# q and k projected into 32-row groups per head, split in place, with the scores in pairs of row groups

## What is computed

```
h = group_norm(x, 32 groups of 4 channels) * gn_w + gn_b
q, k, v = wq @ h + bq, wk @ h + bk, wv @ h + bv
attn = softmax(q_head.T @ k_head * scale)      # 256 x 256 per head
x = wp @ (v_head @ attn.T, heads joined) + bp + x
```

## Time and profile before

| | |
|---|---|
| runs (us) | 115.32, 118.06, 115.12; median 115.32 |
| span of the profiled execution (us) | 112.7; its own time is not reported beside it |
| median of the runs less the span (us) | 2.6 |
| busy TensorE, VectorE, ScalarE (us) | 99.7, 77.9, 78.4 |
| TensorE instructions | 774 matmuls, each with a weight load |

### The profile page before, as it was taken

One profiled execution on the slowest core, in us unless ns is written; L12 is line 12 of the kernel. 1 busy time (PEld: TensorE's weight loads), 2 busy tenths in 40 slices (PEclk: granted clock), 3 DMA queues, 4 the chain that ended last, 5 costly groups with the idle time before them and its releaser, 6 DMA issues.

```text
span 112.7 us, 2178 instructions
## 1 busy us (share of the span) xinstructions
PE 99.7 (88%) x774; PEld 80.1 (71%) x774; DVE 77.9 (69%) x192; ACT 78.4 (70%) x168; POOL 7.9 (7%) x17
## 2 busy tenths in 40 slices
PE   6999689979969998599999899979998898789891
PEld 6998468756955967378877678768977565579770
DVE  5467789273992879826699357997869516786862
ACT  4387569998677937989828996377999995024520
POOL 8421000000001000010000100010000000102000
PEclk9999999999999999999999999999999999999998
DMA  2950000000000000000000000000000000000011
GB/s 65 333 214 0 0 0 6 0 0 0 3 9 0 0 0 0 0 0 6 0 0 0 0 6 0 0 0 0 6 0 0 0 0 9 0 3 0 0 47 47
DMA packets 1882, 2.12 MB, mean 19 GB/s; under 512 B 336, under 2 KB 1232, under 8 KB 1872
## 3 DMA queue, kind: packets, MB, share of 16 engines
q1 hardware_dynamic: 1584, 1.84, 4.8%
q10 hardware_dynamic: 288, 0.15, 0.6%
HBM read 1.73 MB, written 0.26 MB: 18 GB/s over the span
## 4 chain that ended last, share of the span: by engine, by line
PE 58%; ACT 20%; DVE 14%; issue 4%; DVEq 0%; ACTq 0%
ACT probs L668 9%; PE ps_o L563 9%; PE ps_t L550 9%; ACT q_heads L658 8%; PE ps_w L492 7%; PE ps_o L469 6%; DVE neg_max L761 6%; PE ps_w L520 4%; PE ps_w L510 4%; PE ps_w L511 3%; PE ps_m L498 2%; DVE q_heads L755 2%; PE ps_m L537 2%; PE ps_m L477 2%; PE ps_m L609 2%
## 5 line engine op out<-in xcount | busy, mean ns | idle before, releaser
L761 DVE TENSOR_REDUCE neg_max<-ps_w 128x2 f32<-128x512 f32 x48 | 31.0, 685 | 6.8 <-PE ps_w L520 6.7
L668 ACT ACTIVATE probs<-ps_t 128x512 f32<-128x512 f32 x48 | 27.5, 597 | 4.1 <-PE ps_t L550 3.3
L550 PE MATMUL ps_t<-q_heads,k_pairs 128*128 128x256 f32 x96 | 20.8, 313 | 3.1 <-ACT probs L668 1.6
L520 PE MATMUL ps_w<-k_pairs,q_heads 128*128 128x256 f32 x96 | 20.4, 314 | 1.8 <-DVE neg_max L761 0.8
L658 ACT ACTIVATE q_heads<-ps_m 1x256 fp32r<-1x256 f32 x48 | 17.9, 373 | 5.0 <-PE ps_m L537 4.1
L550 PEld LDWEIGHTS ps_t<-q_heads,k_pairs 128*128 128x128 f32 x96 | 14.1, 189 | 7.0 <-ACT q_heads L658 4.3
L520 PEld LDWEIGHTS ps_w<-k_pairs,q_heads 128*128 128x128 f32 x96 | 13.9, 189 | 5.5 <-issue 2.4
L510 PE MATMUL ps_w<-qk_high,select 128*128 128x256 f32 x48 | 12.9, 300 | 0.9 <-DVE qk_low L726 0.5
L563 PE MATMUL ps_o<-probs,v_heads 128*32 128x256 f32 x192 | 12.8, 385 | 0.9 <-ACT probs L668 0.9
L511 PE MATMUL ps_w<-qk_low,select 128*128 128x256 f32 x48 | 11.8, 279 | 0.0
L423 POOL TENSOR_TENSOR grp<-grp,const 128x1 f32<-128x1 f32 x8 | 4.5, 558 | 93.8 <-DVE grp L715 93.8
(11 more groups left out here) (62 smaller groups left out, 130.2 us busy)
## 6 DMA issues: line engine op xcount, KB each, us to landing
w<-in_w SPq DMA_DIRECT2D x4, 256.0 KB, 4.9
xs<-in_x SPq DMA_DIRECT2D x2, 128.0 KB, 3.1
selections<-in_selections SPq DMA_DIRECT2D x1, 256.0 KB, 4.0
out<-xs SPq DMA_DIRECT2D x4, 64.0 KB, 1.6
const<-in_constants ACTq DMA_DIRECT2D x1, 137.0 KB, 3.1
vec<-in_vectors ACTq DMA_DIRECT2D x1, 12.0 KB, 3.5
```

Source lines behind the costliest of these rows:

```text
L520: last = mm(ps_w[w_slot[step]][:, qc * T:(qc + 1) * T], q_heads[b][:, i, qc * CHUNK:(qc + 1) * CHUNK], k_pairs[b][:, i // 2, :], start=Tru ...
L550: last = mm(dst, k_pairs[b][:, pair, keys], q_heads[b][:, i, :], start=True, stop=True)
L668: nc.scalar.activation(probs[:, i, :, :].rearrange("p c t -> p (c t)"), src, ACT.Exp, scale=SCALE).then_inc(exps_done, 1)
L761: nc.vector.tensor_reduce(neg_max[b][:, i // 2, :, QUAD * (i % 2)], ps_w[w_slot["scores", l, b, i]][:, :].rearrange("p (c t) -> p c t", c= ...
```

## The change

Instead of one q and one k projection there are two of each (`SETS`), on weights whose columns are repeated: a set holds four heads, each in its own group of 32 rows, and the 16 rows of a head stand in it twice. q is split in place: ScalarE writes the rounded value in the second 16 rows and zero in the first (`mask_q`), and VectorE subtracts that from q (`split_q`), which leaves the full value, rounded, in the first 16 rows and the remainder in the others. k is split into a high and a low tile as before, per set. The placing matmuls, their stores and the selection matrices are gone.

The scores of two heads are now one step of 8 matmuls of 32 rows, which alternate between two row groups and two PSUM banks (high and low part of k, two query halves). The scores by keys are a step of 12 such matmuls, where the last two of each half multiply a row of ones with the stored maxima. The maxima of four heads are turned and stored together, in one store of 128 partitions. There is one ring of five PSUM banks, `probs` exists per image, v is stored by ScalarE, and the plan's table has other times; `fold_bias` is no longer in `LANDED`.

```diff
-WORK, SLOTS = 3, 2
+RING = 5
...
-LANDED = {("moments", 0, 0, 0): 3., ("scale_w", 0, 0, 0): 4.5, ("group_means", 0, 0, 0): 4.5,
-          ("variance", 0, 0, 0): 5.4, ("fold_bias", 0, 0, 0): 6.6, ("moments", 0, 1, 0): 5.8}
+LANDED = {("moments", 0, 0, 0): 3.5, ("scale_w", 0, 0, 0): 4.7, ("group_means", 0, 0, 0): 4.4,
+          ("moments", 0, 1, 0): 5.6}
...
+                for n in range(SETS):
+                    for kind, before in (("mask_q", "project"), ("round_k", "project"),
+                                         ("split_q", "mask_q"), ("split_k", "round_k")):
+                        step(kind, n, (before, n), *[(kind, n - 1)] * n)
+                    for kind in ("mask_q", "round_k"):
+                        needs[kind, l, b, n].append(("add_bias", l, 0, 0))
+                    step("turn_max", n, ("store_v", 0), *[("row_max", PER * n + j) for j in range(PER)],
+                         *[("store_max", n - 1)] * n)
+                    step("store_max", n, ("turn_max", n))
...
+                step("project_v", 0, ("project", SETS - 1))
+                for p in range(PAIRS):
+                    step("scores", p, ("split_q", p // 2), ("split_k", p // 2), *[("scores", p - 1)] * min(p, 1))
+                    step("scores_t", p, ("store_max", p // 2), *[("scores_t", p - 1)] * min(p, 1))
+                    for h in (2 * p, 2 * p + 1):
+                        step("row_max", h, ("scores", p), *[("row_max", h - 1)] * min(h, 1))
+                        step("exps", h, ("scores_t", p), *[("exps", h - 1)] * min(h, 1))
...
+            banks = emptied_by(step)
+            for j in range(len(banks)):
+                if len(ring) + j >= RING:
+                    awaited.append(ring[len(ring) + j - RING])
...
+                        for n, first in enumerate((W_Q[l], W_K[l])):
+                            ring_free(step, n)
+                            mm(slot(step, n)[:, 0:T], ws[l][:, first + i, :], hn[b][:, :],
+                               start=True, stop=True).then_inc(qk_projected, 1)
...
-                elif kind in ("place_q", "place_k"):
-                    k = int(kind == "place_k")
-                    pe.wait_ge(qk_split, nth("split", l, b, k))
-                    if l == 0:
-                        pe.wait_ge(select_ready, (i + 1) * PAIRS // STACKS)
-                    ring_free(step)
-                    for n in range(2):
-                        dst = ps_w[w_slot[step]][:, n * T:(n + 1) * T]
-                        pair = 2 * i + n
-                        mm(dst, select[:, pair, 2 * k, :], qk_high[b][:, k, :], start=True, stop=False)
-                        last = mm(dst, select[:, pair, 2 * k + 1, :], qk_low[b][:, k, :], start=False, stop=True)
-                    last.then_inc(k_placed if k else q_placed, 1)
...
+                    s = i // 2
+                    pe.wait_ge(q_ready, nth("split_q", l, b, s))
+                    pe.wait_ge(k_ready, nth("split_k", l, b, s))
+                    for j in range(2):
+                        ring_free(step, j)
                     for qc in range(NCH):
-                        last = mm(ps_w[w_slot[step]][:, qc * T:(qc + 1) * T],
-                                  q_heads[b][:, i, qc * CHUNK:(qc + 1) * CHUNK], k_pairs[b][:, i // 2, :],
-                                  start=True, stop=True)
+                        for n, keys in enumerate((k_high, k_low)):
+                            for j in range(2):
+                                r = QUAD * (2 * (i % 2) + j)
+                                last = mm(slot(step, j)[:, qc * T:(qc + 1) * T],
+                                          q_split[b][r:r + QUAD, s, qc * CHUNK:(qc + 1) * CHUNK],
+                                          keys[b][r:r + QUAD, s, :], start=(n == 0), stop=(n == 1))
...
-                    pe.wait_ge(max_done, nth("row_max", l, b, 2 * i + 1))
+                    pe.wait_ge(max_done, nth("row_max", l, b, PER * (i + 1) - 1))
...
+                    s = i // 2
+                    pe.wait_ge(max_stored, nth("store_max", l, b, s))
+                    if l == 0:
+                        pe.wait_ge(ones_ready, 1)
+                    for j in range(2):
+                        ring_free(step, j)
...
+                        for n, part in enumerate((k_high, k_low)):
+                            for j in range(2):
+                                r = QUAD * (2 * (i % 2) + j)
+                                mm(slot(step, j)[:, kc * T:(kc + 1) * T], part[b][r:r + QUAD, s, keys],
+                                   q_split[b][r:r + QUAD, s, :], start=(n == 0), stop=False)
+                        for j in range(2):
+                            r = QUAD * (2 * (i % 2) + j)
+                            last = mm(slot(step, j)[:, kc * T:(kc + 1) * T], ones[r:r + 1, :],
+                                      max_rows[b][r:r + 1, s, :], start=False, stop=True)
...
+                elif kind == "mask_q":
+                    act.wait_ge(bias_ready, nth("add_bias", l, 0))
+                    act.wait_ge(qk_projected, 2 * nth("project", l, b, i) - 1)
+                    nc.scalar.activation(q_low[b][:, i, :], slot(("project", l, b, i), 0)[:, 0:T], ACT.Identity,
+                                         bias=bias_low[:, l, i:i + 1], scale=low_rows).then_inc(q_masked, 1)
+                elif kind == "round_k":
+                    act.wait_ge(bias_ready, nth("add_bias", l, 0))
+                    act.wait_ge(qk_projected, 2 * nth("project", l, b, i))
+                    nc.scalar.activation(k_high[b][:, i, :], slot(("project", l, b, i), 1)[:, 0:T], ACT.Identity,
+                                         bias=bias[:, l, K_BIAS + i:K_BIAS + i + 1]).then_inc(k_rounded, 1)
...
-                elif kind == "store_q":
-                    act.wait_ge(q_placed, nth("place_q", l, b, i))
-                    if l == 0:
-                        act.wait_ge(zeros_ready[b], 1)
-                    src = ps_w[w_slot["place_q", l, b, i]][0:HALF, :].rearrange("p (n t) -> p n t", n=2)
-                    nc.scalar.activation(q_heads[b][0:HALF, PER * i:PER * (i + 1):2, :], src,
-                                         ACT.Copy).then_inc(q_stored_even, 1)
-                elif kind == "store_k":
-                    act.wait_ge(k_placed, nth("place_k", l, b, i))
-                    dst = k_pairs[b][:, 2 * i:2 * i + 2, :].rearrange("p n t -> p (n t)")
-                    nc.scalar.activation(dst, ps_w[w_slot["place_k", l, b, i]][:, :], ACT.Identity,
-                                         bias=ones_rows).then_inc(k_stored, 1)
...
-                    for odd in range(2):
-                        row = HALF * odd + MAX_ROW
-                        last = nc.scalar.activation(q_heads[b][row:row + 1, 2 * i + odd, :],
-                                                    m[QUAD * odd:QUAD * odd + 1, 0:T], ACT.Copy)
-                    last.then_inc(max_stored, 1)
+                    nc.scalar.activation(max_rows[b][:, i, :], m[:, i * T:(i + 1) * T],
+                                         ACT.Copy).then_inc(max_stored, 1)
...
+                    link(tt(bias[:, l, :], slot(step_of_fold(l))[:, 0:NBIAS], vec[:, l, BQ:BV + 1], ALU.add))
+                    ts(bias_low[:, l, :], bias[:, l, Q_BIAS:Q_BIAS + SETS], low_rows, None,
+                       ALU.mult).then_inc(bias_ready, 1)
...
+                elif kind == "split_q":
+                    dve.wait_ge(q_masked, nth("mask_q", l, b, i))
+                    stt(out=q_split[b][:, i, :], in0=slot(("project", l, b, i), 0)[:, 0:T],
+                        scalar=bias[:, l, Q_BIAS + i:Q_BIAS + i + 1], in1=q_low[b][:, i, :].bitcast(F32),
+                        op0=ALU.add, op1=ALU.subtract).then_inc(q_ready, 1)
+                elif kind == "split_k":
+                    dve.wait_ge(k_rounded, nth("round_k", l, b, i))
+                    stt(out=k_low[b][:, i, :], in0=slot(("project", l, b, i), 1)[:, 0:T],
+                        scalar=bias[:, l, K_BIAS + i:K_BIAS + i + 1], in1=k_high[b][:, i, :].bitcast(F32),
+                        op0=ALU.add, op1=ALU.subtract).then_inc(k_ready, 1)
```

464 lines of the change are left out of this document (191 added, 273 removed).

## The result

The changed kernel takes 143.19 us (median of 4 runs, 142.39 to 145.86) against 116.62 for the kernel before on the same chip: the ratio is 1.242, with an interval of 1.230 to 1.255. It is slower by 24%. The prediction said 116.2 us with a range of 108.5 to 122.5, so it is wrong, by 27 us.

The account below looks back on a forecast made before the run. The prediction saw no engine full, but many short steps handed between engines, with TensorE 58% of the chain. Removed work of -18.5 us and added terms came to +0.9, giving 116.2 us, range 108.5 to 122.5.

Parts of the forecast that it names:

- The pace of TensorE: TensorE's cost per instruction, read from the earlier trace: 0.12 us for a matmul of 256 columns in fp32r.
- The start: Kernel start: the fold waits for the first weights, with fillers behind it, so the first row maximum comes 2.6 us later.
- The wait for four maxima: The turn of the maxima waits for four row maxima instead of two; two sets counted in full, +2.4 us.
- A change of shape: At the scores, 75 changes of matmul shape instead of 24, each 0.10 us on TensorE: +3.3 us.
- term 5: Scores by keys: 12 matmuls per pair of heads in 6 slots if two row groups run side by side, +5.1 us.
- the stores of the maxima: On ScalarE, 48 one-partition stores become 12 of 128x256, taken at 450 ns each: -6.3 us.
- slots of scores stretched by 1.3: Inside the serial row-group case: if row tiles overlap only partly, score slots stretch by 1.3 and the time is near 121.
- Row groups one after another: Rival at the scores: row groups don't overlap, each matmul takes its own slot; 120 to 136 us, chance 0.13.
- TensorE's list blocks: Rival: the wait for four maxima and the bank ring hold up TensorE's later work; 121 to 123 us, chance 0.21.
- No change: The sum of terms as it stands, 113.0 to 117.6 us; chance 0.36.
- faster: Rival: ScalarE's relief counts in full and covers waits and start; 107 at best, 110 in the middle, chance 0.30.
- slower: Both slower rivals together, serial row groups and a blocked TensorE list: over 2% slower, chance 0.34.

Follow-up runs that it names:

- a_full: The changed kernel with each side-by-side pair of 32-row matmuls replaced by one matmul over all 128 rows in the same slots, heads mixed: 121.74 us.
- a_64: The changed kernel with each pair of 32-row matmuls replaced by one matmul over the same 64 rows, heads mixed: 139.41 us.
- a_one: The changed kernel with only one 32-row matmul in each slot where it has two side by side: 152.69 us.
- b_64: The kernel before, with its scores and scores by keys contracted over the first 64 rows only: 131.29 us.
- b_32: The kernel before, with its scores and scores by keys contracted over the first 32 rows only: 159.69 us.
- a_start_pm: The changed kernel with the fold back at its old place and the maxima turned and stored per two heads: 125.18 us.
- a_full_start: The changed kernel with 128-row matmuls in the same slots, heads mixed, and the fold back at its old place: 117.38 us.
- a_full_start_pm: The changed kernel with 128-row matmuls, heads mixed, the fold at its old place and maxima turned and stored per two heads: 114.39 us.
- a_full_chg: The changed kernel with 128-row matmuls in the same slots, plus one tiny 32-row matmul ahead of each of the 48 score steps: 130.37 us.
- a_start: The changed kernel with only the fold put back at its old place, behind the fillers and both group means: 142.80 us.
- b_wait: The kernel before, with one more 128x512 copy on ScalarE ahead of every second exp: 128.21 us.
- a_quad_start: The changed kernel with the fold at its old place and four heads' scores in one step, four row groups side by side: 145.51 us.
- a_fill: The changed kernel with one filler matmul of 128x128 zeros ahead of each of the 48 scores and scores-by-keys steps: 162.53 us.

## Why the prediction was wrong

**The step that failed is "The pace of TensorE".** It read 0.12 for a matmul of 256 columns from the earlier trace rows and priced every later term with it. That figure belongs to full clock. The trace of before has no matmul of 32 rows at all, and the bounds that were asked for it were only whether two row groups overlap; whether TensorE keeps its clock with them was not asked, and no rival had it. The runs show the mean clock at 0.805 in its place, 54.9 us of the span at the half level, where the slot is 0.21. Of the 27 us of error that is the greater part, some 16 to 22: 22 is the estimate from the stretch at 65.84, and 21.5 is the distance to a_full, of which 53 changes of shape at 0.094 may be 5. That it is due to the rows shows in a_full, a_64, a_one (121.7, 139.4, 152.7 in the same slots) and in b_64 against b_32 (131.3, 159.7), without any of the change's other parts. How deep it falls depends on the waits as well: a_start_pm, with the same rows, is back at 0.902.

**The terms at full clock.** That 113.3, the span less the most that the half level can have cost, agrees with 113.6 is luck. a_full has the change's order at a clock of 0.972 and no changes of shape at its scores; the forecast without that term is 116.2 - 3.3 = 112.9, and it took 121.7, of which at most 3.4 is its own half level. Three terms were too small, by 4 to 7 us together:
- The start (+2.6) is worth 4.4 to 5.0 by a_full_start: the fold and the fillers run at 0.21 from cold, and the fold waits for the vectors until 5.2.
- The wait for four maxima (+2.4) is worth 3 to 5.4 by a_full_start_pm at 128 rows, with the dearer stores of the alternative already in.
- A change of shape (6) costs 0.10 at both of the two gaps behind it, of which only one was read from the earlier trace rows. By a_full_chg 51 changes at 0.094 are 4.8 us of time, where +3.3 was taken.

Other terms came out as read, or near it:
- Pairs of row groups take one slot of 0.12 (term 5): shown by the starts.
- ScalarE and VectorE came out at 58 and 72 us; the stores of the maxima are 384 ns, not 450, so 0.8 us of ScalarE better in all.
- a_full_start_pm has neither the late start, nor the wait for four, nor the changes of shape, and 12 turns and 12 stores more. By the prediction's own terms it should take 116.2 - 2.6 - 2.4 - 3.3 + 1.1 + 2.3 = 111.3 (2.3 is 12 stores of 0.384 at the half that stores had on the chain). Its runs took 110.6 to 117.5, so the terms for the work that was removed and added aren't contradicted.
- Two slips don't decide: the median less the span is 1.8 in the change (142.5 - 140.7), where 2.6 was taken, and slots of scores stretched by 1.3 give 116.2 + 0.3 x 20 = 122, not 121.

**The rivals.** Row groups one after another: out. TensorE's list blocks: this wait does count, but through the clock. a_start_pm, which takes it away, is 17.6 us faster than a_start, and still lies 6 us over before at best; the rival had priced it at 5 to 7 us at full clock. "No change" and "faster" both assumed the pace. The chance of slower, 0.34, was right in sign without the mechanism that decided.

**What stays open.** How waits and few rows act together: b_wait loses little clock at 128 rows, while a_start_pm gains 18 us over the change from fewer waits with the same rows, and a_start, which also takes a wait away, gains nothing. And why four groups of 32 rows side by side (a_quad_start), or a filler between the steps (a_fill), don't hold the clock.

## What to carry to other kernels

When a change swaps matmuls of 128 rows for ones of 32 or 64, price TensorE at both levels of its clock and give the half level a chance of its own, above all where TensorE is 88% of the span; row groups side by side can lose more on the clock than the placing work that they make needless. And take waits and rows together: an order that keeps 32-row matmuls waiting cost 17.6 us here where it cost 3 to 5 with 128 rows. Zeros in unused rows are not waste there: the kernel before carries half of its rows as zeros and runs at full clock. Read the granted clock line before any share of busy time, since a TensorE that is always busy may be so because it is slow.

## What the runs showed of the hardware

- With the order of steps kept, the granted clock followed the rows that the matmuls contract over: 0.984 to 0.999, 0.928 and 0.687 for 128, 64 and 32 rows of the scores in the kernel before, and 0.972, 0.814 and 0.734 in the change's order. Zero weights in 128 rows: 0.976. Rows are not all of it: with the change's own rows and two waits less (start and maxima) the clock was 0.902 (a_start_pm), and with four groups of 32 rows at once 0.826 (a_quad_start).
- The clock fell from full to half behind a stretch in which TensorE had no gap (a_start_pm, 15.6 to 19.0 us, nearly all matmuls of 32 rows or one), and held behind one that was busy for 2.64 of 3.40 us with 128 rows (a_full, 21.0 to 24.4).
- Fewer rows made a kernel slower with less work: a_one leaves out half of the score matmuls of the change and takes 9.5 us more.
- Two 32-row matmuls in different row groups and banks start within 10 ns of each other and share one slot of 0.12 us (0.21 at the half level), with weight loads of 128 columns for each. The Trainium skill, "TensorEngine Tiling (Array Packing)", When to Use Tiling, recommends row tiling for a contraction of 64 rows or fewer; the slots agree. Against one 32-row matmul per slot the pair is the better choice (143.19 against 152.69 us in a_one, with twice the work); against 128 rows of which half are zeros the kernel lost (1.242).
- A change between shapes costs 0.10 us ahead of the first matmul and another 0.10 ahead of the second; 92 more of them left the clock where it was (0.972 and 0.973).
